# Work taken off GpSimd in the mixer's opening, transfers on two queues, thirty unread transposes before the rows return, and one zero matmul per read-out

## What is computed

```python
def _L1_attn_ref(x, ...):              # ETA = 0.1, DT = 0.01, 8 heads of 64
    pot = layernorm(x) @ w_pot + b_pot
    V, gamma = pot[..., 0], softplus(pot[..., 1]) + 0.1
    d = complex(V + 2.0, -gamma)       # tridiagonal matrix, off-diagonal -1
    a = _cf_scan(d)                    # a_i = d_i - 1/a_{i-1}, along the rows
    b = _cf_scan(d[:, ::-1])[:, ::-1]
    G = 1.0 / (a + b - d)
    x = x + stack([G.real, G.imag]) @ w_bk + b_bk
    q, k, v = split(layernorm(x) @ w_qkv + b_qkv)
    # W = exp(-gamma_t*DT) * W + ETA * outer(k_t, v_t);  out_t = q_t @ W
    x = x + hebbian_scan(q, k, v, gamma) @ w_out + b_out
    return x + gelu(layernorm(x) @ w_ff1 + b_ff1) @ w_ff2 + b_ff2
```

## Time and profile before

| | us |
|---|---|
| median of 3 runs | 2057.92 |
| lowest, highest | 2056.25, 2060.32 |
| the profiled execution, its own time | 2059.54 |
| its span, first to last instruction | 2057.7 |
| mixer block, from its first instruction to the last of its main loop | 911.4 to 1249.6 |
| PE: bias products of `w_qkv` (first 2.4 us at 2.4 GHz, the rest at 1.2), turning the potentials | 929.6 to 938.0, 938.0 to 939.8 |
| PE: bias products of `w1`, running sums of gamma | 939.8 to 946.8, 957.0 to 964.0 |
| ACT: from the running sums to the last exponential (`dec`) | 958.0 to 969.6 |

### The profile page before, as it was taken

The page is one execution under the profiler, slowest core; times in us unless marked ns, Lnnn a source line. Parts: engine busy times, 40 slices in busy tenths (PEclk is TensorE's granted clock), DMA queues, the critical chain, the costliest instruction groups (busy, mean ns, idle before and its releaser), DMA issues. The chain is left out here.

```text
span 2057.7 us, 28609 instructions
## 1 busy us (share of the span) xinstructions
PE 1559.1 (76%) x9916; PEld 1293.0 (63%) x9916; DVE 1088.6 (53%) x2181; ACT 905.4 (44%) x1589; POOL 906.6 (44%) x704
## 2 busy tenths in 40 slices
PE   4787888889689738835089997976880699999990
PEld 1565665677568738824058877955870588878880
DVE  7667868678669612346654444448644123322222
ACT  4697887989344415514042234533341122323220
POOL 0598796998433246635001135030005106593406
PEclk8899999999899859965579999998985799999995
DMA  3001011011110224330000000020045102332003
GB/s 116 21 22 42 21 42 42 22 42 42 67 29 1 115 95 154 118 113 26 1 1 1 1 1 1 1 83 1 1 156 185 47 29 88 104 132 90 29 19 122
DMA packets 51961, 114.47 MB, mean 56 GB/s; under 512 B 13997, under 2 KB 34378, under 8 KB 44277
## 3 DMA queue, kind: packets, MB, share of 16 engines
q1 hardware_dynamic: 45060, 84.67, 11.8%
q0 software_dynamic: 6768, 28.02, 4.1%
HBM read 87.02 MB, written 25.87 MB: 55 GB/s over the span
## 5 line engine op out<-in xcount | busy, mean ns | idle before, releaser
L855 POOL TENSOR_TENSOR HC<-H,CB 128x512 f32<-128x512 f32 x256 | 322.2, 1282 | 108.7 <-DVE H L755 93.7
L432 PE MATMUL ps<-ident,UT 128*128 128x128 f32 x1024 | 167.3, 288 | 36.7 <-ACT UT L586 18.6
L755 DVE TENSOR_TENSOR_SCAN H<-dA,ps 128x512 f32<-128x512 f32 x128 | 152.9, 1213 | 79.3 <-PE ps L432 70.6
L586 ACT ACTIVATE UT<-DTXT,BT 128x512 f32<-128x512 f32 x256 | 181.4, 710 | 29.9 <-PE ps L432 29.5
L432 PEld LDWEIGHTS ps<-ident,UT 128*128 128x128 f32 x1024 | 124.2, 147 | 103.3 <-DVE H L755 38.4
L596 ACT ACTIVATE dA<-DT,nA 128x512 f32<-128x512 f32 x256 | 181.4, 710 | 11.4 <-DVE H L755 8.6
L441 PE MATMUL ps<-ident,HC 128*128 128x128 f32 x1024 | 160.2, 285 | 31.6 <-POOL HC L855 29.7
L755 DVE TENSOR_TENSOR_SCAN H<-dA,HL,ps 128x512 f32<-128x512 f32 x128 | 158.0, 1268 | 37.2 <-PE ps L432 31.8
L441 PEld LDWEIGHTS ps<-ident,HC 128*128 128x128 f32 x1024 | 123.2, 147 | 42.4 <-POOL HC L855 41.7
L2003 DVE TENSOR_TENSOR f_XN<-f_XN,ps 128x1024 f32<-128x1024 f32 x39 | 47.7, 1222 | 174.9 <-PE ps L153 174.9
L1779 POOL TENSOR_TENSOR f_W<-f_stage,f_zeros 128x2048 fp32r<-128x2048 f32 x18 | 64.9, 3607 | 167.8 <-POOLq L1796 167.4
(11 more groups left out here) (499 smaller groups left out, 4282.3 us busy)
## 6 DMA issues: line engine op xcount, KB each, us to landing
CB<-m_c_rows SPq DMA_DIRECT2D x16, 1024.0 KB, 4.7
f_w<-in_f_w SPq DMA_DIRECT2D x16, 1024.0 KB
f_stage<-in_f_w POOLq DMA_DIRECT2D x15, 1024.0 KB, 5.5
f_stage<-in_f_w SPq DMA_DIRECT2D x9, 1024.0 KB
f_rows_in<-f_zeros SPq DMA_DIRECT2D x13, 384.0 KB, 12.2
f_DI<-f_rows_in SPq DMA_DIRECT2D x39, 128.0 KB, 2.2
f_rows_out<-f_EO SPq DMA_DIRECT2D x39, 128.0 KB, 1.7
a_values<-a_zeros SPq DMA_DIRECT2D x8, 320.0 KB, 5.5
```

What stands on the lines that cost most here:

```text
L432: ins = pe.transpose(PS[4 + G % UR][:, t * P:(t + 1) * P], UT[:, n % 2, t, c * P:(c + 1) * P], g.ident[:, :])
L586: act.activation(UT[:, N % 2, t, :], DTXT[:, k % 2, t, :], ACT.Copy, scale=BT[:, k % 2, t, n:n + 1]).then_inc(ut_ready, 1)
L755: dve.tensor_tensor_scan(H[:, G % HR, :], dA[:, G % AR, :], PS[4 + G % UR][:, :], first, ALU.mult, ALU.add).then_inc(h_ready, 1)
L855: pool.tensor_tensor(HC[:, y, :], H[:, s, :], CB[:, n // 4 % CR, n % 4, :], ALU.mult).then_inc(hc_ready, 1)
```

## The change

**POOL** keeps only the scaling of `w_pot`, some clearing of memory and one subtraction of 16 columns. The low halves `l_qkv` and `l_out` are made on DVE, where one operation now scales and subtracts. The scaling of `w1` goes to ACT. The masking of `DM` goes to DVE in four pieces; the factor ETA leaves the mask and the key scale and goes into `h_out` and `l_out`. What stood on POOL, before and now, from the start of the mixer to its first `h_QS`:

PE changed between 64 and 128 columns of the array four times in each direction, and now does so once. The diff follows, cut to this; `spread_potential`, `spread_start` and `gather_green` split the transfers to `CH`, `A0` and `GR` as `gather_matrices` splits those to `Q`:

```diff
+        def gather_matrices(q, half):
+            for b in range(B):
+                lo_ = 64 * half + NC * b
+                q.dma_start(Q[32 * half + b:32 * half + b + 1, :, :, :, :].rearrange("a c x y z -> a c (x y z)"),
+                            MM[lo_:lo_ + NC, :, :, :].rearrange("p x y z -> p (x y z)")).then_inc(q_loaded, 16)
...
@@ block.sync
+                spread_potential(s, 0)
...
+                gather_matrices(s, 0)
...
+                spread_start(s, 0)
...
+                gather_green(s, 0)
@@ block.gpsimd
-                pool.wait_ge(wb_ready, 1)
-                pool.wait_ge(wh_ready, KD + 1)
+                pool.wait_ge(xt_ready, NT)
...
@@ block.tensor
+                pe.wait_ge(xt_ready, NT)
+                pe.wait_ge(pot_copied, 4)
+                for t in range(NT):
+                    ins = pe.transpose(PS[0][:, 2 * t:2 * t + 2], POT[:, t * P:(t + 1) * P], g.ident[0:2, 0:2])
+                ins.then_inc(potT_ready, 1)
                 pe.wait_ge(w_loaded, W_ALL)
...
-                pe.wait_ge(ub_added, 1)
                 pe.wait_ge(gamma_ready, 1)
...
+                pe.wait_ge(ub_added, 1)
+                pe.wait_ge(aa_ready, 1)
+                for n in range(30):
+                    pe.transpose(PS[0][:, 0:P], g.ident[:, :], g.ident[:, :])
                 pe.wait_ge(gr_loaded, 32)
...
+                    pe.matmul(PS[6][:, :], zero[:, :], zero[:, 0:1].to_broadcast([1, NP * P]), start=True, stop=False)
                     for q in range(NP):
                         for h in range(2):
                             pe.matmul(PS[6][h * HDW:(h + 1) * HDW, q * P:(q + 1) * P], VV[:, r, q * P + h * HDW:q * P + (h + 1) * HDW],
-                                      PTm[:, r, h * NP + q, :], start=True, stop=False)
-                        ins = pe.matmul(PS[6][:, q * P:(q + 1) * P], WS[:, q, :], QS[:, r, q, :], start=False, stop=True)
+                                      PTm[:, r, h * NP + q, :], start=False, stop=False)
+                    for q in range(NP):
+                        ins = pe.matmul(PS[6][:, q * P:(q + 1) * P], WS[:, q, :], QS[:, r, q, :], start=False, stop=(q == NP - 1))
@@ block.scalar
+                act.wait_ge(pot_copied, 4)
+                spread_potential(act, 1)
...
+                act.wait_ge(ub_ready, 1)
+                for k in range(KD):
+                    act.activation(w.w1[:, k, :], w.w1[:, k, :], ACT.Copy, scale=w.g3[:, k:k + 1]).then_inc(up_scaled, 1)
+                act.activation(var1[:, 0:1], Lt[:, 0:1], ACT.Sqrt)
+                act.wait_ge(ones_ready, 2)
+                act.wait_ge(mm_ready, 1)
+                gather_matrices(act, 1)
+                act.wait_ge(ia_ready, 1)
+                spread_start(act, 1)
+                act.wait_ge(gg_ready, 1)
+                gather_green(act, 1)
@@ block.vector
-                dve.wait_ge(wb_ready, 1)
-                dve.tensor_tensor(b_qk[:, :], b_qk[:, :], PS[1][:, 0:2 * PAIRS], ALU.add).then_inc(wb_added, 1)
-                dve.tensor_tensor(b_v[:, :], b_v[:, :], PS[2][:, :], ALU.add).then_inc(wb_added, 1)
-
                 dve.wait_ge(ch_loaded, 64)
                 dve.wait_ge(potT_ready, 1)
...
                 dve.sem_inc(sp_in, 1)
-                dve.wait_ge(ub_ready, 1)
-                dve.tensor_tensor(w.bf1[:, :], w.bf1[:, :], PS[3][:, 64:64 + FC], ALU.add).then_inc(ub_added, 1)
+                low_qkv(0)
...
+                dve.wait_ge(dm_out, 1)
+                for j in range(2):
+                    mask_decay(j)
                 dve.wait_ge(b2_loaded, 16)
```

More of the change, by code:

```diff
@@ L2122, in mixer_core @@
         DM = sb("DM", [P, NT, P])
-        mask = sb("mask", [P, P])
+        zero = sb("zero", [1, P], BF16)
         w_bk = same_place(nc, "h_w_bk", [3, D], F32)
@@ L2198, in _ @@
                 s.wait_ge(gg_ready, 1)
-                for r in range(2):
-                    s.dma_start(GR[r:r + 1, :].rearrange("a (p i) -> a p i", i=CL), GG[:, r, :]).then_inc(gr_loaded, 16)
+                gather_green(s, 0)
             @block.gpsimd
@@ L2205, in _ @@
                 pool.memset(WS[:, :, :], 0.0).then_inc(ws_clear, 1)
-                pool.tensor_scalar(mask[:, :], g.upper[:, :], ETA, None, ALU.mult).then_inc(pool_chain, 1)
+                pool.memset(zero[:, :], 0.0).then_inc(ws_clear, 1)
                 pool.wait_ge(loaded, ALL)
@@ L2320, in _ @@
                     ins.then_inc(lb_ready, 1)
+                pe.wait_ge(late_loaded, U_ALL)
+                pe.wait_ge(sp_in, 1)
+                for f in range(FC):
+                    for kd in range(KD):
+                        ins = pe.matmul(PS[0][:, 64 + f:65 + f], w.w1[:, kd, f * P:(f + 1) * P], w.b3[:, kd:kd + 1],
+                                        start=(kd == 0), stop=(kd == KD - 1))
+                ins.then_inc(ub_ready, 1)
                 def forward(t):
@@ L2689, in _ @@
                 dve.sem_inc(ia_ready, 1)
+                dve.wait_ge(wh_ready, KD + 1)
+                dve.scalar_tensor_tensor(l_out[:, :, :], w.w_out, ETA, h_out[:, :, :].bitcast(F32),
+                                         ALU.mult, ALU.subtract).then_inc(wl_ready, 1)
+                dve.wait_ge(ub_ready, 1)
+                dve.tensor_tensor(w.bf1[:, :], w.bf1[:, :], PS[0][:, 64:64 + FC], ALU.add).then_inc(ub_added, 1)
                 dve.wait_ge(a0_loaded, 64)
@@ L2726, in _ @@
                 dve.sem_inc(gg_ready, 1)
+                for j in range(2, 4):
+                    mask_decay(j)
                 def correct(t):
```

67 lines of the change are left out of this document (24 added, 43 removed).

## The result

The changed kernel takes 2027.28 us at the median (2025.83 to 2030.72, 4 runs), the kernel before 2058.82 (2056.25 to 2060.32, 4 runs) beside it: a ratio of 0.985, 95% interval 0.9833 to 0.9868. That is 31.5 us less, faster by more than the 0.2% that a measurement can tell, and inside the range of 2013 to 2034. The forecast was 2022.4. The profiled execution was the longest of the four, 2030.72 us around a span of 2029.0, so the two traces differ by 28.7 us.

A forecast was written before the change was run, and what follows sets the result against it. It took DVE's chain of small operations, with its waits, to bound the opening and PE the main loop. Terms A to F sum to 35.5 us, off the median of 2057.92 us: forecast 2022.4 us, range 2013 to 2034.

The forecast's parts named there:

- A: Opening, potentials to gamma: inputs come earlier and DVE's 8.94 us operation shrinks to some 0.2; 16.1 us less.
- B: DVE's first chain: its line no longer held by POOL takes 7.1 us in place of 12.9; 5.8 us less.
- C: Hand-overs at Q and A0: two issues on each of two queues start the last transfer sooner; 1.1 and 1.2 us less.
- D: From AA to the first forward product: split issues, thirty transposes ending with the transfer; 0.2 us less, between 0.55 and -0.9.
- E: Rows' return, forward products: transposes raise PE's clock, which falls back within a few us; 0.7 us less, at least 0.
- F: Main loop's read-out: three of four column changes go, a zero product is added; 0.65 us each, 10.4 us in all.
- Rival 1: The raised clock stays up through the rows' return, giving 4.8 us in place of 0.7; 2018.3 us; chance 0.14.
- Rival 2: Transposes do not raise the clock, so D is -0.9 and E 0; 2024.2 us; chance 0.06.
- Rival 3: The new order inside the read-out gives nothing and the zero product stays; 2032.8 to 2036.5 us; chance 0.10.
- Rival 5: Slower than before: adding into an already opened bank makes PE finish each read-out product first; 2087 us; chance 0.03.

The follow-up runs named there:

- E5: Changed kernel plus one unread POOL sum of 1024 columns beside DVE's first chain, which DVE also waits for before the mask; 2032.66 us, one run.
- E6: Changed kernel with all transfers of the potentials, Q, A0 and the Green's function issued by SP, none by ACT; 2027.51 us, ratio 0.9861.
- E3: Changed kernel with three unread 512-column products behind each of the first seven forward products, and a wait for h_qkv; 2035.59 us, ratio 0.9887.
- E1: The changed kernel run once more with no edit; 2026.76 us, ratio 0.9847.
- E7: Changed kernel with DVE's first two mask products moved from before its wait for B2 to behind the Green's function values; 2026.77 us, one run.
- E8: Kernel before the change, with only the new read-out order and its zero product added; 2047.08 us, ratio 0.9947.
- E12: E11 with the read-out's four state products first, the first opening the bank, and no zero product; 2021.63 us, ratio 0.9825.
- E2: Changed kernel without the thirty unread transposes; 2027.43 us, ratio 0.9851.
- E4: Changed kernel with the old order inside the read-out of each tile and no zero product; 2041.03 us, ratio 0.9914.
- E9: Changed kernel with twelve more unread transposes in front of TensorE's wait for AA; 2021.96 us, ratio 0.9832.
- E10: E9 with the first two query products of the rows' return back to back, the others one a round; 2023.24 us, ratio 0.9838.
- E11: E9 with the first three query products of the rows' return back to back, the others one a round; 2021.14 us, ratio 0.9828.

## Why the prediction was right, and where its terms were off

| step | predicted | by the traces |
|---|---|---|
| A, to gamma | 16.1 | 16.48 |
| B, first chain | 5.8 | 5.79 |
| C, `Q` | 1.1 | 0.11 |
| C, `A0` | 1.2 | 0.42 |
| D, `AA` to forward | 0.2 | -1.17 |
| E, forward to first query product | 0.7 | 0.51 |
| return of the rows from there | none | -5.58 |
| F, loop and its end | 10.4 | 10.1 + 2.0 |
| sum | 35.5 | 28.7 |

- **A and B** held in size. B and 8.7 us of A came out of one reading, that large POOL operations hold DVE's small ones, and E5 shows it. The rest of A, the input that comes earlier because PE turns the potentials first, is read from the timeline (ACT waited 6.65 us for it before, and now DVE waits for ACT); no run took it alone.
- **C** was mis-sized. The step that failed is "four issues took 2.49 us; with two on each queue the last one starts 1.25 us sooner": it does start sooner and the last packet moves 0.9 to 1.0 us sooner, but the landing is reported 0.85 to 1.1 us behind that packet in place of 0.3 (E6), so DVE got going only 0.1 to 0.4 us sooner. The bound of 1.25 above and 0 below held.
- **D** had the wrong thing late. The step said that the transposes and the transfer of `GR` end together; they did not meet at all (transposes done at 1005.28, forward at 1006.78). What came was a load of TensorE's program on top of `B2`'s transfer, 1.5 us, which nothing in the profile of before pointed to at this place. At -1.17 the term lies outside its bound of -0.9; the split of `GR`'s issues gave 0.31 of its 0.55.
- **E** held: the transposes raised the clock, it fell back within a few us, 0.51 us for 0.7. Rival 1 fell with the clock at 0.50 from 1007.6, and in E3 dense filling did not hold it either. Rival 2, the rule that transposes do not raise the clock, fell in eleven profiles.
- **The return of the rows** is the term that the sum lacked. I took the 3 us at 0.50 behind the first query product from the one trace of before as fixed. It was 11.5 to 16.1 us in the eight profiles of the changed kernel and E1 to E7, at a cost of 3.6 to 5.7 us, and 3.3 to 3.7 in E8 to E12. It is not the transposes (E2), nor the read-out (E4, E8), nor the queues (E6), nor the masks (E7). The clock records of the traces show what it goes with. In each profile all changes of the granted clock (50 to 62 of them) lie whole multiples of one shortest distance apart, so they mark a grid in time. Where the first query product starts in that grid sorts all fourteen profiles:

| first query product starts, us behind a point of the grid | clock back after, us | profiles |
|---|---|---|
| -0.3 to 0.1 | 3.3 to 3.7 | before, E8, E9, E10, E11, E12 |
| 1.0 to 1.3 | 15.8 to 16.1 | changed kernel, E2, E3, E5 |
| 1.4 to 2.2 | 11.5 to 12.3 | E1, E4, E6, E7 |

The changed kernel and E1 are one program and stand in two of the rows. So the early return of the kernel before was a lucky place in the grid, the change lost it, and E9 got it back without meaning to. This is a sorting of fourteen profiles: no run moved that start and nothing else, and why the late returns take 11.5 or 16 us is not shown. Differences of 3.6 to 5.7 us between totals can come from this alone, which may be part of why the runs of E3 spread over 13 us and those of E9 over 7.
- **F** was right in cause and a little small: 0.73 us a tile for 0.65, 11.7 in all for 10.4. The mis-sized part is the zero product, 0.31 us (1145.73 to 1146.04) for the forecast's 0.40, and E12 gets it back, 0.30 of a tile; 0.73 + 0.31 = 1.04 us for three changes of columns is the forecast's 1.05. Rivals 3 and 5 fall with E4 and E8.

The forecast came out 4.9 us low at the median. In the profiled execution, the longest of the four, the two terms that were missing, D's load and the late clock, cost 7.0 us and C gave 1.8 us less than forecast, against 2.1 us that A and F gave more. That the measured time is still inside the range is in part luck: the range was made wide for rivals 1, 2 and 3, none of which came, and it happened to hold an error that no term or rival named.

## What to carry to other kernels

Where a chain of small DVE operations sets the time, look for the one of them that is twenty times as long as its like, and see whether a POOL operation ends with it: moving POOL's work was worth the whole excess here. When unread instructions are added to an engine's program, look in the list of transfers for where its instruction packets fall, before and after, and keep them off the transfer that somebody waits for. Where TensorE never waits, products of one shape belong in a row, and a bank can be opened by a product that is needed anyway. Before a difference of a few us in the total is put down to an edit, look at where the granted clock changed in both profiles.

## What the runs showed of the hardware that was not expected

- A packet of an instruction queue (16 KB, 0.96 to 1.45 us) held the last 5 of 80 packets of a 16 KB transfer back until it had ended, in seven profiles; the receiver got going 1.3 to 2.0 us later (3.17 to 3.83 for 1.85).
- A row of query products and forward products on TensorE brought the granted clock from 0.50 to 1.00 after 3.3 to 3.7 us in six profiles and after 11.5 to 16.1 us in eight, sorted without exception by where their start lay in the grid of the clock's changes; in E3 PE was busy without a gap for 17.0 us and again for 15.2 us at 0.50.
- Two issues of a transfer took ACT 1.46 to 1.51 us and SP 1.19 to 1.23. With four transfers on two queues the last landing was reported 0.85 to 1.1 us behind the last packet, with four on one queue 0.3.
- A DVE operation of four columns was held to the end of POOL's operation on two inputs (2.27 of 2.35 us, 4.41 of 4.50) but for only 0.90 and 1.11 us beside POOL's scalings of 2.84 us.
